# Causal mask of the first attention pass moved from TensorE matmuls into a fused VectorE operation

## The reference

```python
x = L0_attn_x
xn = _layernorm(x, axis=-1)
x = x + _L0_attn_ref(xn, ...) + _L0_ffn_ref(xn, ...)

# in _L0_attn_ref: 16 heads of 8 features, rotary q and k, a distance bias
scores = jnp.einsum('bhqd,bhkd->bhqk', q_rot, k_rot) / jnp.float32(math.sqrt(dh))
...
scores = scores + decay_bias[None]
causal = jnp.tril(jnp.ones((n, n), dtype=bool))
scores = jnp.where(causal[None, None], scores, jnp.float32(-jnp.inf))
attn = jax.nn.softmax(scores, axis=-1)
out = jnp.einsum('bhqk,bhkd->bhqd', attn, v)
```

## Time and profile before

| | |
|---|---|
| median of 3 runs | 1587.77 us (1586.25 to 1587.83) |
| the profiled execution | 1589.88 us, of which its span is 1588.1 us |
| PE busy | 1350.6 us, 85% of the span |
| DVE busy | 1135.8 us, 72% |
| ACT busy | 794.9 us, 50% |
| POOL busy | 362.2 us, 23% |

### The profile page before, as it was taken

How to read it: one execution, slowest core, us unless ns; L and a number is a source line. 1 busy time by engine, 2 the same in 40 slices (tenths; PEclk the granted TensorE clock), 3 DMA queues, 4 the chain that set the end, 5 groups by cost and what they waited for, 6 DMA issues and landing times.

```text
span 1588.1 us, 35422 instructions
## 1 busy us (share of the span) xinstructions
PE 1350.6 (85%) x10534; PEld 1023.0 (64%) x10628; DVE 1135.8 (72%) x4601; ACT 794.9 (50%) x1688; POOL 362.2 (23%) x454
## 2 busy tenths in 40 slices
PE   0279999999999999999999999999995588888887
PEld 0157777777777777777777777777773255555555
DVE  8657777777777777777777777778644577777761
ACT  1136555555565565555555656555563244443442
POOL 3011222111112211111122111112211233333332
PEclk9679999999999999999999999999997699999999
DMA  4412332323223333232232333223310332233332
GB/s 106 91 50 69 82 77 75 98 68 78 68 71 80 75 80 93 68 78 68 71 80 74 90 83 78 68 68 79 76 42 11 114 133 102 107 126 133 132 134 81
DMA packets 86696, 133.22 MB, mean 84 GB/s; under 512 B 9162, under 2 KB 77114, under 8 KB 77370
## 3 DMA queue, kind: packets, MB, share of 16 engines
q1 hardware_dynamic: 86098, 132.10, 29.5%
q10 hardware_dynamic: 488, 0.01, 0.0%
HBM read 108.76 MB, written 21.50 MB: 82 GB/s over the span
## 4 chain that ended last, share of the span: by engine, by line
PE 41%; DVE 29%; issue 13%; DMA 7%; ACT 5%; DVEq 3%; SPq 1%; POOL 1%; ACTq 0%; POOLq 0%
DMA qst<-mT 6%; PE ps L1355 4%; PE ps L1365 4%; PE ps L1356 4%; PE ps L1564 3%; PE ps L1229 3%; PE ps L1400 3%; DVE mx L995 3%; PE ps L1333 3%; DVEq L823 2%; PE ps L1556 2%; PE ps L1314 2%; DVE ats L1156 2%; PE ps L1291 1%; ACT n1s L777 1%
## 5 line engine op out<-in xcount | busy, mean ns | idle before, releaser
L652 ACT ACTIVATE pr<-ps 128x512 f32<-128x512 f32 x384 | 227.5, 593 | 188.7 <-PE ps L1314 160.9
L995 DVE TENSOR_REDUCE mx<-ps 128x2 f32<-128x512 f32 (+1 forms) x384 | 262.6, 685 | 49.8 <-PE ps L1291 25.4
L657 ACT ACTIVATE ps<-trn 128x512 f32<-128x512 bf16 x382 | 229.8, 601 | 12.2
L520 POOL TENSOR_TENSOR zt<-xn,bmv 128x256 f32<-128x256 f32 x32 | 19.6, 614 | 823.3 <-DVE rstd L101 823.3
L514 POOL TENSOR_TENSOR n1s<-rep,n1T 128x256 f32<-128x256 f32 x256 | 177.3, 731 | 113.0 <-DVE mpart L1007 88.8
L1564 PEld LDWEIGHTS ps<-w2s,ats 128*128 128x128 f32 x1024 | 127.2, 191 | 92.2 <-DVE ats L1156 47.0
L1564 PE MATMUL ps<-w2s,ats 128*128 128x128 f32 x1024 | 140.5, 280 | 34.4 <-DVE ats L1156 26.3
L1355 PE MATMUL ps<-n1s,wq 128*128 128x256 f32 x512 | 160.5, 395 | 0.0
L777 ACT ACTIVATE n1s<-ps 128x512 f32<-128x512 f32 x128 | 76.5, 598 | 157.9 <-PE ps L1556 156.6
L1356 PE MATMUL ps<-n1s,wk 128*128 128x256 f32 x512 | 152.7, 380 | 0.0
L1365 PE MATMUL ps<-wv,n1s 128*128 128x128 f32 x1024 | 150.6, 280 | 0.0
(11 more groups left out here) (221 smaller groups left out, 2632.3 us busy)
## 6 DMA issues: line engine op xcount, KB each, us to landing
rep<-scr_rw SPq DMA_DIRECT2D x32, 1024.0 KB, 5.1
qst<-scr_rw SPq DMA_DIRECT2D x8, 2048.0 KB, 7.6
kst<-scr_rw SPq DMA_DIRECT2D x8, 2048.0 KB, 7.5
scr_parts<-parts SPq DMA_DIRECT2D x64, 192.0 KB, 2.3
qst<-scr_parts SPq DMA_DIRECT2D x192, 64.0 KB
kst<-scr_parts SPq DMA_DIRECT2D x32, 192.0 KB
xt<-in_x SPq DMA_DIRECT2D x32, 128.0 KB, 2.4
kst<-scr_parts SPq DMA_DIRECT2D x32, 128.0 KB
```

The source lines that it names most:

```text
L652: act.activation(pr[:, G % 2, i], ps[:, S2[k % 2]], ACT.Exp).then_inc(exp_done, 1)
L657: act.activation(ps[:, S2[k % 2]], seeds[:, 1 if (k + 2) % 3 == 2 else 0], ACT.Copy).then_inc(seed_done, 1)
L995: dve.tensor_reduce(mx[:, min(i, 1), h:h + n], ps[:, S1[k % 2]].rearrange("p (h t) -> p h t", h=n), AX_X, ALU.max, negate=True).then_inc(s ...
```

## The change

The eight two-head units and four four-head units of a sequence no longer begin with a mask matmul: the first score matmul of each slice overwrites instead. DVE adds the mask: `row_max` is now one `tensor_tensor_reduce` per head. It adds the mask to the head's scores, multiplies by -1, writes the result back over the scores in PSUM and writes the minimum along the row to `mx` as an accumulator output. A four-head unit has four of them, over 128 columns each, a two-head unit has two over 256 columns. `s1_read` is raised by the last one. The mask lies in `theta` as `mask_w`, filled by two more DVE instructions in the setup: 128 columns of zero and 128 columns of the causal mask. The mask matmul of the single-head attention (`soft_scores`, L1374) stays. DVE's loop over steps 2 to 27 is written out by Python; the loops of the other engines stay.

```diff
--- before.py
+++ after.py
@@ -208,6 +208,7 @@
         prf = pr[:].rearrange("p a i t -> p (a i t)")
         bt = prf[:, 0:2 * TM * D].rearrange("p (a i c) -> p a i c", a=2, i=TM)
         seeds = trn[:].rearrange("p a t -> p (a t)").bitcast(BF16).rearrange("p (k t) -> p k t", k=2)
+        mask_w = theta
         z2 = prf[:, 2 * TM * D:3 * TM * D].rearrange("p (i c) -> p i c", i=TM)
         rep2 = [v[:].rearrange("p a h t -> p (a h t)").bitcast(F32).rearrange("p (e t) -> p e t", e=E)
                 for v in (qst, kst)]
@@ -321,7 +322,7 @@
         block = ctx.enter_context(nc.Block())
         N_CONST, N_W, N_SMALL = 13, 8, 5
         N_ROWS = 18
-        SIN_READY, N_SET_DVE = 18, 56
+        SIN_READY, N_SET_DVE = 18, 58
         UP, MOE = (0, 1, 2), (3, 4)
 
 
@@ -890,6 +891,8 @@
 
             for h in range(HG):
                 ch.add(dve.tensor_copy(mask_qk[:, h], mask_in[:, 0]))
+            ch.add(dve.memset(mask_w[:, 0:P], 0.0))
+            ch.add(dve.tensor_copy(mask_w[:, P:S], mask_in[:, 0]))
             ch.link(dve.memset(seeds[:, 0], 0.0))
             for h in range(2):
                 ch.add(dve.tensor_copy(seeds[:, 0, S * h:S * h + P], mask_in[:, 1]))
@@ -992,8 +995,12 @@
                     dve.wait_ge(max_chain, (MAX_LINKS + 1) * b)
                 n = HG if i == 0 else 2
                 h = HG * G + (0 if i < 2 else 2)
-                dve.tensor_reduce(mx[:, min(i, 1), h:h + n], ps[:, S1[k % 2]].rearrange("p (h t) -> p h t", h=n),
-                                  AX_X, ALU.max, negate=True).then_inc(s1_read, 1)
+                w = 2 * S // n
+                for j in range(n):
+                    scores = ps[:, S1[k % 2], w * j:w * j + w]
+                    ins = dve.tensor_tensor_reduce(scores, scores, mask_w[:, S - w:S], -1.0, 3.0e38, ALU.add, ALU.min,
+                                                   mx[:, min(i, 1), h + j:h + j + 1])
+                ins.then_inc(s1_read, 1)
 
             def max_parts(b):
                 c = Chain(dve, max_chain, b, MAX_LINKS + 1)
@@ -1119,7 +1126,7 @@
             max_parts(0)
             step(0, 0, 3)
             step(1, 1, 3)
-            with dve.Fori(1, NB // 2 - 2) as j:
+            for j in range(1, NB // 2 - 2):
                 for u in range(2):
                     step(2 * j + u, u, 3)
             step(NB - 4, 0, 3)
@@ -1277,19 +1284,15 @@
                 pe.wait_ge(s1_read, UNITS * b + max(k - 1, 0))
                 bank = ps[:, S1[k % 2]]
                 if i == 0:
-                    mm(bank, identb[:], mask_qk[:].rearrange("p h t -> p (h t)"), start=True, stop=False,
-                       skip_group_check=True)
                     for h in range(HG):
                         hh = HG * G + h
                         ins = mm(bank[:, h * P:(h + 1) * P], qst[0:KR, par, hh, 0:P], kst[0:KR, par, hh, 0:P],
-                                 start=False, stop=True, skip_group_check=True)
+                                 start=True, stop=True, skip_group_check=True)
                 else:
-                    mm(bank.rearrange("p (h t) -> p h t", h=2)[:, :, P:S], identb[:], mask_qk[:, 0:2],
-                       start=True, stop=False, skip_group_check=True)
                     for h in range(2):
                         hh = HG * G + 2 * (i - 1) + h
                         ins = mm(bank[:, h * S:(h + 1) * S], qst[0:KR, par, hh, P:S], kst[0:KR, par, hh, :],
-                                 start=False, stop=True, skip_group_check=True)
+                                 start=True, stop=True, skip_group_check=True)
                 ins.then_inc(s1_out, 1)
 
             def max_T(b):
```

## The result

The changed kernel takes 1610.51 us (1610.22 to 1610.90) against 1587.80 beside it: a ratio of 1.0148, 95% interval 1.0133 to 1.0163. It is slower by 22.7 us; the forecast was 51. The direction held and the time lies inside the range, but the loss was put at more than twice its size. The profiled execution has a span of 1609.1 us against 1588.1, 21.0 more.

What follows compares the result with a forecast made beforehand. A step was taken as a ring: PE up to unit 2, DVE to `normalise`, then PE. Looped steps +41.3, steps 0, 1 and 28 +7.0, step 30 -1.7, first pass +3.8, setup +0.4: +50.8 us, so 1639 us, range 1600 to 1718.

Steps and rivals of the forecast that it cites:

- The ring: Each step: PE up to unit 2, DVE from there to `normalise`, PE from `att_T` on; only what lies on it counts.
- Masks off PE: Mask matmuls dropped from PE: only those of units 0, 1 and 2 count, a gain of 0.43 us a step.
- The DMA wait: PE's wait for the DMA that brings the maxima is covered when DVE is late: 0.32 us a step gained.
- The written-out loop: DVE from unit 2 to unit 9 loses what the loop adds between instructions: 0.73 us a looped step gained.
- The fused operation without its output: DVE's units cost as reduces of the same columns: 0.80 us for a four-head unit, 0.67 for a two-head unit.
- The price of an accumulator output: On DVE, r for delivering each fused operation's minimum: taken as 0.08 us, between 0 and 0.18; 26 outputs a step count.
- the prediction's own formula: The whole kernel's change as a function of r, with 786 outputs on the path: -12.1 + 786 r us.
- r = 0: Rival: DVE's accumulator output is free, written by the same instruction; 1576 us, faster; chance 0.14.
- a read as dear as on ACT: Rival: DVE's read waits for the operation before it, r = 0.18; 1717 us; chance 0.20 for 1675 and above.
- PE as the bound: Rival: every mask matmul on PE counts, 53 us less, 1535 us; chance 0.02.
- the cancelling case: Rival: costs and gains cancel over the kernel, r near 0.015; 1588 us; chance 0.04.
- The start: Before the loop: setup copies +0.4 us, first pass of sequence 0 +3.8, step 0 +2.32.

Runs made afterwards that it cites:

- e2: e1 without the mask matmuls of the first pass, DVE keeping its one reduce a unit; 1553.61 us, ratio 0.9780.
- e4: The changed kernel with the fused operation only in units 0 and 1, mask matmuls and one reduce in units 2 to 11; 1565.58 us, ratio 0.9857.
- e5: The changed kernel with the fused operation only in units 2 to 11, mask matmul and one reduce in units 0 and 1; 1619.65 us, ratio 1.0203.
- e8: The kernel before with every loop of both phases and all engines written out and nothing fused; 1560.01 us, ratio 0.9837.
- e1: The kernel before with only DVE's loop over steps 2 to 27 written out; 1571.48 us, ratio 0.9890.
- e3: The changed kernel with a plain add of the mask for each fused operation, row maxima left out; 1578.67 us, ratio 0.9940.
- e9: e4 with the loops of both phases on all engines written out, run again beside e8; 1549.51 us, ratio 0.9772.

## Why the prediction was wrong in size

**The ring: right.** DVE from unit 2 to `normalise`, PE around it. e2 (PE's savings behind unit 2 are worth nothing), e4 and e5 (the same edit is a gain ahead of unit 2 and a loss behind it) show it.

**Masks off PE, 0.43 us: right.** e2 has 0.46 in the mean, and the shortest times to unit 2 have 9.44 in e8 and 9.01 after, 0.43. **The DMA wait, 0.32 us: right in kind, too small.** To unit 2 the two together were forecast at 0.75 and measured at 9.91 - 9.16 = 0.75, but the equality is chance: writing out DVE's loop makes this stretch 0.16 longer (e1), which the prediction had left out. From e1's 10.07 to 9.16 are 0.91, less 0.46 for the masks 0.45. PE's wait for the DMA fell from 7.9 us (9.2 in e1) to 1.3. The cause named was that a late DVE lets `max_T` run some 0.4 us earlier against `att_T`; the rows above show 0.36 (0.19 to 0.55). No run moves `max_T` alone, so that this is what ends the wait is not shown.

**The written-out loop, 0.73 us: a little too much.** The looped steps alternate, 14.46 us in one and 14.23 in the other, and I had read only the first kind: 14.35 on average, so 0.62. That is 26 x 0.11 = 3 us, in the other direction from the miss. The prediction named waits computed from registers as the only thing that the loop can add; no run tests that.

**The fused operation without its output: right.** 0.80 and 0.67 us forecast, the same in e3. By the 120 cycles of the Trainium skill's page ("VectorE: DVE Perf Modes", the errata), an estimate for four operations of 128 columns is 4 x 0.258 = 1.03 us and for two of 256 columns 2 x 0.392 = 0.78. As with the row of before, the trace does not agree on the time from start to start; the durations recorded for one operation, 0.28 and 0.41 us, lie within 0.03 of the page's.

**The price of an accumulator output, r = 0.08 us: this is the term that failed.** It measures 0.042 (1.10 / 26 in e3; 0.037 in the units alone). I took the spacing of two-element operations for that of a read, as if a read held DVE like an operation of its own. The rows after show that the next operation starts with it, and what is left is 0.03 to 0.04 us more until the start after. The 26 outputs of a step at 0.038 less are 0.99 us, somewhat more than what separates the period forecast, 36.8, from the 35.95 measured. With r = 0.042 the prediction's own formula gives -12.1 + 786 x 0.042 = +20.9 us; measured are +21.0 in the spans and +22.7 in the medians. The rivals: r = 0 (1576 us) falls by e3, a read as dear as on ACT falls by the same rows, PE as the bound falls by e2, and the cancelling case would have needed a price of 0.015.

**Smaller terms.** Step 28 grew by 35.62 - 33.87 = 1.75 us (forecast 2.32, with r = 0.042 it is 1.33). Step 29 became 34.11 - 33.07 = 1.04 us shorter where I had put nothing, and step 30 did not change (30.36 and 30.48) where I had put -1.7: without the layer norm of step 28 beside it, step 29 leaves DVE room, and in step 30 the room was less than the one idle of 0.78 us made me believe. That is my reading; no run tests it. Together these are 1 us more than with r = 0.042.

**The start: forecast too dear.** With r = 0.042 the formula has 4.3 us for the setup, the first pass of sequence 0 and step 0. The two executions reach the end of step 0 at 133.80 and 133.92 us, 0.12 apart. The first pass of sequence 0 itself, to `max_parts`, grew from 93.11 - 84.24 = 8.87 us to 92.37 - 81.95 = 10.42, so by 1.55 and not 2.6; before, DVE waited for PE between its first units there (0.28 and 0.16 us), and some of the growth could fall into these waits. Most of the rest is that its first unit starts 2.3 us earlier, which may be chance: in the other executions step 0 ends anywhere between 132.56 and 136.32 us.

That 20.9 and 21.0 agree so closely is luck. The 26 steps grew by 19.1 us where the formula has 15.7; the loop's 3 us too many and 2.6 us of slow clock (below) push that way. The start, 4.2 us below the formula, hides it.

## What to carry to other kernels

Busy shares called this kernel bound by PE, yet three quarters of the saved PE time bought nothing. Find in each step where one engine hands over to the other, and ask of every piece of an edit on which side of that point it falls; then keep the half that pays, as e9 does. And where an operation is not in the trace, the spacing of starts is the price, not the duration of its parts: the 141 ns of a read cost some 40.

## What the runs showed of the hardware

**A read of the accumulator overlaps what follows it on DVE.** Its successor is recorded with the same start in the rows above; 1024 reads with 144.9 us of busy time cost some 33 us in the end (the changed kernel against e3), with 2.6 us of slow clock in it.

**TensorE's clock dipped where it had not before.** Over steps 3 to 27 the mean granted clock was 1.00 before and is 0.99 after. In six of the 26 steps (4, 7, 17, 20, 22 and 24) it is 0.95. A stretch of 3 us in step 17 (length, busy times of PE, PEld, DVE, ACT and POOL, then the granted clock):

```profile
735.00:738.00 3.00, 3.00 (x24) 1.93 (x23) 2.74 (x18) 0.42 (x2) 1.43 (x3) 0.50 0.55 131
```

For some 3 us PE ran at 1.2 in place of 2.4 GHz. In this step and in step 4 that began just after PE had waited 0.66, 1.11 and 0.61 us for DVE's maxima within 5 us, and the step's last part took 6.05 and 5.99 us in place of 5.06. In the other four it began some 2 us earlier, just behind the second of these waits, and cost 0.14 to 0.23 us. Together that is 2.6 us. e5_units2_11, the other kernel with as much waiting for DVE, has such steps too (four of the 26, and step 1), the rest of the experiments have none. The 20 other steps of the changed kernel have the same three waits (in one of them the first is 0.99) and no dip, so what sets it off stays open.

**A hardware loop costs DVE time between its instructions**, 0.62 us in 14.35 here, in every iteration and not only at its end. Set beside e1, some 20 of the 71 operations between the starts of units 2 and 9 have a successor that starts 20 to 45 ns later in the loop, nearly all of them short ones whose own spacing is under 0.1 us in e1. In every second step one more spacing, behind L949, is 0.23 us longer; this is why the steps alternate. What in the loop does it is not shown.
